# Attention and lookup layer on one core: loops written out, first loads reordered, v projected in one run, and weighted values taken for two key tiles at every second step

## What is computed

```python
q, k, v = (jnp.moveaxis(qkv, 2, 0)[i] for i in range(3))        # (1, 16, 4096, 16) each
scores = jnp.einsum('bqhd,bkhd->bhqk', q, k) * scale
attn = jax.nn.softmax(scores, axis=-1)
out = jnp.einsum('bhqk,bkhd->bqhd', attn, v).reshape(B, N, C)
```

## Time and profile before

| | |
|---|---|
| time, median of 3 runs | 3265.24 us (3263.46 to 3269.75) |
| profiled execution, its own time | 3264.68 us |
| its span (first to last instruction) | 3262.9 us |
| busy share of the span | PE 95%, DVE 87%, ACT 77%, POOL 8% |
| chain that ended last | PE 93%, DVE 2%, issue 2%, ACT 1%, DMA 1% |
| attention, first score to last weighted values | 191.8 to 2857 us |

### The profile page before, as it was taken

The page is one execution under the profiler, slowest core; times in us unless marked ns, Lnnn a source line. Parts: engine busy times, 40 slices in busy tenths (PEclk is TensorE's granted clock), DMA queues, the critical chain, the costliest instruction groups (busy, mean ns, idle before and its releaser), DMA issues.

```text
span 3262.9 us, 80910 instructions
## 1 busy us (share of the span) xinstructions
PE 3107.3 (95%) x26983; PEld 1366.9 (42%) x26983; DVE 2833.9 (87%) x3108; ACT 2504.8 (77%) x4551; POOL 260.8 (8%) x810
## 2 busy tenths in 40 slices
PE   8799999999999999999999999999999999988883
PEld 3444443344344434443444344434434444456652
DVE  5389999999999999999999999999999999456666
ACT  6158888888888888888888888888888888733333
POOL 2300000000000000000000000000000000011103
PEclk9689999999999999999999999999999999989996
DMA  7700101010101011000101010101010100000001
GB/s 259 88 1 1 34 8 28 14 27 14 25 17 24 18 21 21 21 21 15 27 14 27 12 30 11 30 8 34 8 34 8 34 9 22 1 1 0 0 0 52
DMA packets 27390, 83.30 MB, mean 26 GB/s; under 512 B 4641, under 2 KB 15633, under 8 KB 24018
## 3 DMA queue, kind: packets, MB, share of 16 engines
q1 hardware_dynamic: 26818, 77.84, 10.7%
q0 software_dynamic: 272, 1.05, 0.1%
HBM read 57.90 MB, written 20.97 MB: 24 GB/s over the span
## 4 chain that ended last, share of the span: by engine, by line
PE 93%; DVE 2%; issue 2%; ACT 1%; DMA 1%; POOL 1%; DVEq 0%; SPq 0%; POOLq 0%; ACTq 0%
PE ps L1022 41%; PE ps L1031 36%; PE ps L1239 3%; PE ps L998 3%; PE ps L1188 2%; PE ps L957 2%; PE ps L1041 1%; PE ps L1228 1%; PE ps L971 1%; PE ps L1163 1%; PE ps L1049 1%; PE ps L949 1%; DMA q_stack<-qk_parts 1%; ACT q_raw L619 0%; PE ps L1205 0%
## 5 line engine op out<-in xcount | busy, mean ns | idle before, releaser
L750 DVE TENSOR_REDUCE partial<-ps 128x1 f32<-128x1024 f32 x2048 | 2482.1, 1223 | 179.1 <-PE ps L998 156.0
L569 ACT ACTIVATE work<-ps 128x512 f32<-128x512 f32 x4096 | 2203.3, 597 | 366.3 <-PE ps L1022 151.3
L998 PE MATMUL ps<-k_stack,q_stack 48*128 48x512 f32 x4096 | 1523.2, 451 | 25.2 <-DMA q_stack<-qk_parts 17.0
L1022 PE MATMUL ps<-q_stack,k_stack 64*128 64x512 f32 x4096 | 1513.1, 449 | 21.0 <-issue 19.4
L1031 PE MATMUL ps<-work,v_head 128*32 128x256 f32 x16384 | 1300.9, 392 | 0.0
L1022 PEld LDWEIGHTS ps<-q_stack,k_stack 64*128 64x128 f32 x4096 | 634.8, 185 | 822.2 <-ACT work L569 695.3
L998 PEld LDWEIGHTS ps<-k_stack,q_stack 48*128 48x128 f32 x4096 | 635.4, 187 | 60.9 <-DVE partial L750 32.8
L1031 PEld LDWEIGHTS ps<-work,v_head 128*32 128x32 f32 x16384 | 330.3, 108 | 701.3 <-ACT work L569 575.5
L415 POOL CAST nm_parts<-negmax 128x4 bf16<-128x4 f32 x128 | 24.8, 193 | 2267.5 <-DVE negmax L757 2266.6
L1239 PE MATMUL ps<-k_raw,q_raw 128*128 128x256 f32 x512 | 127.3, 405 | 17.8 <-ACT q_raw L619 17.8
L619 ACT ACTIVATE q_raw<-ps 128x1024 f32<-128x1024 f32 x32 | 32.7, 1023 | 131.5 <-PE ps L1228 131.5
(11 more groups left out here) (128 smaller groups left out, 1110.9 us busy)
## 6 DMA issues: line engine op xcount, KB each, us to landing
k_stack<-qk_parts SPq DMA_DIRECT2D x96, 256.0 KB, 4.2
q_stack<-qk_parts SPq DMA_DIRECT2D x96, 256.0 KB, 4.1
qk_parts<-qk_part SPq DMA_DIRECT2D x32, 512.0 KB, 2.8
x_sb<-L_attn_x SPq DMA_DIRECT2D x8, 512.0 KB, 10.9
out<-work SPq DMA_DIRECT2D x8, 512.0 KB, 2.9
k_raw<-L_ffn_aux_values SPq DMA_DIRECT2D x1, 1024.0 KB
work<-L_attn_w_qkv POOLq DMA_DIRECT2D x1, 768.0 KB, 7.7
q_raw<-L_ffn_aux_keys SPq DMA_DIRECT2D x1, 512.0 KB
```

Source lines behind the costliest of these rows:

```text
L569: act.activation(probs[:, g % DEPTH, a, :], ps[:, bank, :], ACT.Exp, scale=SCALE).then_inc(exp_done, 1)
L750: dve.tensor_reduce(partial[:, k // 4, k % 4:k % 4 + 1], ps[:, 2 * slot:2 * slot + 2, :], AX.XY, ALU.max).then_inc(max_used, 1)
L998: last = pe.matmul(ps[:, 2 * slot + e, :], q_stack[HALF:HALF + ROWS, b1, c * CH + (k // 4) * P:c * CH + (k // 4 + 1) * P], k_stack[HALF:HA ...
L1022: pe.matmul(ps[:, bank, :], k_stack[0:HALF, b, P * g:P * (g + 1)], q_stack[0:HALF, b, at:at + CH], start=True, stop=True).then_inc(s_ready, 1)
```

## The change

Four edits. (1) PE's and ACT's loops over heads are written out, 16 heads one after the other, with constants in the waits. (2) SP starts the first transfers when groups 0 and 2 are out, since head 0 needs nothing of groups 1 and 3. First come the 6 of the slots that max tiles read, with a semaphore `first_max_in`, then the 6 that scores read, with `first_score_in`; head 1's 12 are spread over head 0's steps. (3) All 16 calls of `project_v` come before the first max step. (4) Weighted values are taken at odd steps only, for two key tiles at once.

```diff
+            for g in (0, 2, 1, 3):
+                sp.wait_ge(parts_out[g], 16 * (NC + 1))
+                if g == 2:
+                    load_first((3, 4, 5), first_max_in)
+                    load_first((0, 1, 2), first_score_in)
+            load_stack(1, 0, 1 + CREDIT[pv_done])
...
-            def attend_head(h, b):
-                with act.Fori(0, PAIRS - 1) as j:
-                    attend(h * PAIRS + j, (b, j * 2 + 2))
-                attend(h * PAIRS + (PAIRS - 1), (1 - b, 0))
-
-            with act.Fori(0, H // NB - 1) as r:
-                attend_head(r * NB, 1)
-                attend_head(r * NB + 1, 0)
...
+            for it in range(ITS - 1):
+                h, j = (it + 1) // PAIRS, (it + 1) % PAIRS
+                attend(it, ((h + 1) % NB, 2 * j))
...
-            with pe.Fori(0, NC // 4) as c2:
+            with pe.Fori(0, NC // 2) as c2:
...
-                if before:
-                    weighted_values(*before)
+                if before and g % 2 == 1:
+                    tile, of, v_at = before
+                    weighted_values(tile - 1, of, v_at)
+                    weighted_values(tile, of, v_at)
...
-                    step(g, it, b, j, ahead, (g - LAG, it, b) if g > LAG + 1 else None)
-                    if g == LAG + 1:
-                        weighted_values(0, it, b)
-                        weighted_values(1, it, b)
+                    step(g, it, b, j, ahead, (g - LAG, it, b) if g > LAG else None)
...
-            pe.wait_ge(stack_in[1], 16 * LOADS)
+            pe.wait_ge(first_max_in, 16 * LOADS // 2)
...
-                    if k % 4 == 1:
-
-                        project_v(c * 2 + (NC // 2 + k // 8), k // 8, k // 4 % 2)
...
-            with pe.Fori(0, H // NB - 1) as r:
-                next_loaded(r * NB, 1, r + 1)
-                next_loaded(r * NB + 1, 0, r + 2)
-            next_loaded(H - 2, 1, H // NB)
+            for h in range(H - 1):
+                next_loaded(h, (h + 1) % NB, h // NB + 1)
```

More of the change, by code:

```diff
@@ L208, in sandwich_kernel @@
         stack_in = [sem(f"stack_in{b}") for b in range(NB)]
+        first_max_in = sem("first_max_in")
+        first_score_in = sem("first_score_in")
         s_ready = sem("s_ready")
@@ L297, in _, with load_first, load_stack @@
                     sp.dma_start(dst.rearrange("r f t -> f r t"), qk_part[:, g, :, :]).then_inc(parts_out[g], 16)
-            for g in range(4):
-                sp.wait_ge(parts_out[g], 16 * (NC + 1))
-            def load_stack(h, b, after=None):
+            def load_first(slots, done):
+                for n in slots:
+                    for stack, qk, part in ((k_stack, 1, SLOT_K[n]), (q_stack, 0, SLOT_Q[n])):
+                        sp.dma_start(stack[SLOT_ROW[n]:SLOT_ROW[n] + D, 1, 0:T].bitcast(F32),
+                                     parts_dram[qk, part, 0:D, :]).then_inc(done, 16)
+            def load_stack(h, b, after):
                 for n, (row, pq, pk) in enumerate(zip(SLOT_ROW, SLOT_Q, SLOT_K)):
                     for m, (stack, qk, part) in enumerate(((k_stack, 1, pk), (q_stack, 0, pq))):
-                        if after is not None:
-                            sp.wait_ge(pv_done, after + (2 * n + m) * LOAD_EVERY)
+                        sp.wait_ge(pv_done, after + (2 * n + m) * LOAD_EVERY)
                         sp.dma_start(stack[row:row + D, b, 0:T].bitcast(F32), parts_dram[qk, part, h * D:(h + 1) * D, :]
                                      ).then_inc(stack_in[b], 16)
-            load_stack(0, 1)
-            load_stack(1, 0)
+            for g in (0, 2, 1, 3):
[4 more added lines that the diff above has]
+            load_stack(1, 0, 1 + CREDIT[pv_done])
             for h in range(2, H):
@@ L599, in _ @@
                     exponential(g, a, 0)
-            def attend_head(h, b):
-                with act.Fori(0, PAIRS - 1) as j:
-                    attend(h * PAIRS + j, (b, j * 2 + 2))
-                attend(h * PAIRS + (PAIRS - 1), (1 - b, 0))
-            with act.Fori(0, H // NB - 1) as r:
-                attend_head(r * NB, 1)
-                attend_head(r * NB + 1, 0)
-            attend_head(H - 2, 1)
-            with act.Fori(0, PAIRS - 1) as j:
-                attend(j + (H - 1) * PAIRS, (0, j * 2 + 2))
+            for it in range(ITS - 1):
+                h, j = (it + 1) // PAIRS, (it + 1) % PAIRS
+                attend(it, ((h + 1) % NB, 2 * j))
             attend(ITS - 1, None, {17: 0, KG - 1: 1})
@@ L1127, in _ @@
             pe.wait_ge(rows_set, 2)
+            pe.wait_ge(first_score_in, 16 * LOADS // 2)
             for g in range(LAG):
                 step(g, 0, 1, 0, chunks_ahead(1, 0), None)
-            with pe.Fori(0, H // NB - 1) as r:
-                next_loaded(r * NB, 1, r + 1)
-                next_loaded(r * NB + 1, 0, r + 2)
-            next_loaded(H - 2, 1, H // NB)
+            for h in range(H - 1):
+                next_loaded(h, (h + 1) % NB, h // NB + 1)
             def transpose_weights():
```

## The result

The changed kernel takes 3400.86 us (median of 4 runs, 3395.12 to 3402.88), the kernel before 3265.13. The ratio is 1.0409 (95% interval 1.0394 to 1.0425): 4.1% slower. 3377 was forecast, and 3315 to 3415 was the range. The profiled execution took 3402.88 us, with a span of 3400.2.

The account below looks back on a forecast made before the run. PE was taken to bound the kernel, at 1.235 us a step. From 3264.7 us, loops -28.9, start -28.0 and pairs +169.6 gave 3377 us, 3.4% slower; the range was 3315 to 3415.

Parts of the forecast that it names:

- the ring: In attention: score, exponential, fourth score, two key tiles, next score, closed over three banks; 2.64 us against 2.47.
- The price of a pair: Fifteen of 16 pairs an iteration are new, at 0.149 to 0.171 us each: 2.24 to 2.57 us an iteration.
- The lower price: A new pair in attention with an exponential of 0.60 takes 2.615 us, or 0.149 more than two usual steps.
- The sign named beforehand: In the new profile's attention, a pair from first score to first score takes 2.62 to 2.64 us.
- instruction supply: Rival: fetching PE's straight code stalls as the jumps did, so written-out loops bring nothing: 3406 us; chance 0.04.
- Rows of maxima: After steps 15 and 29, ACT's moved row delays the exponential by 0.28 us each: up to 0.56 an iteration, all taken.
- The copy to `o_sb`: At the pair that exists already, ACT's copy falls into idle time: up to 0.19 us back, 0.15 taken an iteration.
- Sum of the pairs: All pair terms in attention: 2.65 us an iteration, times 64 is +169.6 us (134 to 200).
- Loops: Written-out loops remove six jumps back at a mean of 4.81 us: -28.9 us (25.7 to 32.0).
- Start: Before attention, new transfer order and v first: first score at 161.3 to 166.5 and not 191.82, taken -28.0 us.
- Pairing pays: Rival in attention: PE needs 2.14 us for two steps and DVE becomes the bound, 3035 or 3189 us; chance 0.11.
- The clock: Rival in attention: PE's idling in pairs lowers its clock, one episode an iteration costing 102 us: 3479 us; chance 0.05.

Follow-up runs that it names:

- e6: Changed kernel with each exponential taken over 256 of its 512 columns, so half of the exponentials is left out: 3190.19 us.
- e8: Changed kernel with the two waits of each step's first exponential swapped, so the score's wait stands on the exponential itself: 3345.87 us, ratio 1.0248.
- e2: Kernel before with only weighted values taken for two key tiles at once, loops and start as they were: 3427.32 us, ratio 1.0509.
- e1_single: Changed kernel with weighted values one key tile a step again, written-out loops and new start kept: 3209.32 us, ratio 0.9831.
- e3: Kernel before with only PE's and ACT's loops written out: 3242.44 us, ratio 0.9934.
- e11: e1_single with the exponential's two waits in the order of e8: 3192.71 us, ratio 0.9777.
- e9: e1_single with eight calls of `project_v` put back between the max steps, reordered first transfers kept: 3224.15 us, ratio 0.9853.

## Why the prediction was right, and where it was off

**What bounds the kernel, and the ring.** Right, and for its reason. The fourth score is stalled by the exponential of the first, and e6 and e8 move its start by what they take from the ring. It was readable beforehand since the shape stood once in each iteration.

**The price of a pair.** Its term was mis-sized: taken 0.149 above two single steps, measured 2.67 - 2.466 = 0.21. The lower price of 2.615 is right for ACT's looped code (e2) and for the swapped waits (e8). The missing 0.06 is edit 1's, the separate wait instruction, which the prediction costed at nothing. It looked at what written-out code removes and not at where it puts the waits. 15 x 0.06 x 64 = 58 us would have been the correction, and e8 measured 55. The sign named beforehand, a pair of 2.62 to 2.64, didn't come true for this reason.

Part of this came from a wrong premise. The kernel's description and the prediction say that heads 14 and 15 are written out already. That holds for PE alone: ACT runs their iterations in its inner loop too (`with act.Fori(0, PAIRS - 1)` stands in `attend_head`, and the last head has such a loop of its own). So the earlier trace rows can't show what straight code costs on ACT, and it doesn't support the sentences on register instructions and instruction supply there.

**Rows of maxima.** Taken 0.56 an iteration. The pair that begins behind a row takes 187.34 to 190.13, that is 2.79 and 0.12 more than others. But single steps don't hide all of it, as the prediction had it: behind a row two of them take 2.53 in e1_single and 2.50 and 2.48 in the kernel before. So a pair behind a row costs 0.06 more than a usual pair does against e1_single, and 0.10 against the kernel before: 0.12 or 0.2 an iteration, and not 0.56. The row's own 0.2 of PE's time stood in the kernel before as well. The rows here are the timeline, PE's scores and L1049.

```profile
187.02 0.39 PE L1049 MATMUL ps<-ident_bf,nm_parts 128*3 128x128 bf16 x4
187.34 0.50 PE L1022 MATMUL ps<-q_stack,k_stack 64*128 64x512 f32 x1
...
190.13 0.50 PE L1022 MATMUL ps<-q_stack,k_stack 64*128 64x512 f32 x1
```

**The copy to `o_sb`.** The prediction took 0.15 back, since it read the 2.83 of the earlier trace rows as the copy's doing. The copy stands at the same place in the earlier trace rows; the difference is the jump of ACT's inner loop, as shown above. e2 has edit 4, and its copy starts 0.14 after the score instead of 0.27. With the jump, the exponential still comes at 0.75 there and the pair takes 2.82, so moving key tile 31 doesn't help. Edit 1 does: the pair is 2.68 in every iteration of the changed kernel. The saving measured is 0.06.

**Sum of the pairs.** 2.65 an iteration was taken; 44.0 - 41.0 = 3.0 was measured, and e1_single gives 192 us against 169.6. The positions in the iteration, in the mean over iterations without a stall, account for all of it. Against the kernel before, 12 usual pairs cost 0.21 each, the two behind rows 0.31 each, the pair that stood there already gives 0.06 back, and the pair behind `combine` gives 0.04 back instead of costing 0.149. In single steps that last pair was long already (2.71): a max tile starts 0.26 behind its score there (545.23 against 544.97 in e1_single). In pairs it takes 2.67 like the others. So the forecast of the sum is nearer than its terms: +46 us for usual pairs, and +6 for the copy, against -15 for the rows and -12 behind `combine`. That the errors partly cancel is luck.

```profile
544.97 0.50 PE L1022 MATMUL ps<-q_stack,k_stack 64*128 64x512 f32 x1
...
545.23 0.50 PE L998 MATMUL ps<-k_stack,q_stack 48*128 48x512 f32 x1
```

**Loops.** 28.9 were taken. e3 alone saved 23, with 4.5 lost in the iterations; e11 shows that the wait order can account for that. The sentence that ACT's jumps "lie beside PE's" and cost nothing was true of the outer jumps in the kernel before and would have misled anyone who wrote out PE's loop alone. Of the inner ones it was not true: they cost about 0.2 each in two iterations of four.

**Start.** First score 162.88, inside 161.3 to 166.5; 28.9 saved against 28.0. Two parts of its working were off without harm: v in one run ended at 112.1 and not 113.7, and the first six transfers landed near 100 (e9) and not before 97, hidden behind v as the prediction had it.

**Rivals.** Pairing pays: no, the pair of 2.67 is far from 2.525. Its point was well placed, though: a straight line between e6 (2.46, 3190 us) and the changed kernel (2.67, 3401) reaches 3265 at a pair of about 2.53 (estimate). The clock: PE pauses in each of a thousand pairs, and the granted clock stays at 1.00 from 200 to 3000 us. By the Trainium skill's section on psum-queue depth-cycling (TensorE: Matmul & The Clock Gate) it could have swung; the trace doesn't agree for this pattern. Instruction supply: no stall of PE or ACT for "issue" in attention of the straight code is above 1 us.

The Trainium skill (TensorEngine Tiling, Key Properties) says that a change of tiling mode drains TensorE. The time of the key tiles, 1.00 for two together against 2 x 0.57, is in line with that; no run separates the drain from other costs of a change. It decided nothing, since the array had to wait anyway.

## What to carry to other kernels

Before you bunch operations to save switches, count the buffers between the bunch and its consumer: with n buffers the operation n + 1 of a bunch waits for the whole latency of the first, and here that cost more than the switches saved. If the shape that you want stands anywhere in the trace already, read its price there. When an instruction has several waits and lies on a ring, see that the wait that ends last stands on the instruction itself. If several engines jump at the same time, writing out one of them alone brings next to nothing. And before you take a stretch as an example of straight code, see that it is straight on every engine.

## What was not expected of the hardware

- A wait on an instruction of its own ahead of the exponential costs about 0.06 us on ACT (0.59 against 0.54 from score to exponential). Over some thousand passes of the ring that is 55 us.
- A jump back over a body of two heads costs about 3 us of standstill on ACT and on PE alike, each by itself (3.03 to 3.56 and 2.92 to 3.21), and then a stretch at the lower clock level (granted 0.50 from 528 to 532 us in the kernel before, after PE's 3.18).
- ACT's jump back over one iteration delays the next exponential by about 0.2 us (0.75 against 0.53 from score to exponential).
- In the start's max steps PE's clock is granted at 0.55 (changed kernel, no wait ahead of them), 0.60 (e9, a wait of 1.89 us) and 0.61 (kernel before, a wait of 17.03 us).
